# Statistics and normalisation of a stage's first block in the stage before it

## What is computed

```python
x = x + 0.5 * L0_ffn(layernorm(x))    # gated recurrence over the batch, tanh out
x = x + L0_attn(layernorm(x))         # 16 heads, squared softplus scores
x = x + 0.5 * L0_ffn(layernorm(x))    # the same weights again
x = x + 0.5 * L1_ffn(layernorm(x))    # mixture: 8 experts, best 2
x = x + L1_attn(layernorm(x))         # state space layer (SSM)
x = x + 0.5 * L1_ffn(layernorm(x))    # the mixture again

def layernorm(x, eps=1e-05):
    m, v = mean(x, -1), var(x, -1)
    return (x - m) / sqrt(v + eps)

def L0_ffn_step(c, xt):               # c starts as in_c, broadcast
    ft = sigmoid(xt @ wf.T + c @ uf.T + bf)
    it = sigmoid(xt @ wi.T + c @ ui.T + bi)
    gt = tanh(xt @ wc.T + c @ uc.T + bc)
    return ft * c + it * gt

def L1_ffn(x):
    gates = softmax(x @ gate_w.T + gate_b)       # the best 2 of 8 are kept
    return sum(gate * expert(x) for the 2 experts)
```

## Time and profile before

| What | us |
|---|---|
| Median of 3 runs | 1934.23 |
| The profiled execution's own time | 1933.88 |
| Its span, first to last instruction | 1932.1 |
| TensorE busy | 1752.0 (91%) |
| VectorE busy | 1340.6 (69%) |
| ScalarE busy | 1130.9 (59%) |
| GpSimd busy | 901.4 (47%) |

### The profile page before, as it was taken

One profiled execution on the slowest core, in us unless ns is written; L12 is line 12 of the kernel. 1 busy time (PEld: TensorE's weight loads), 2 busy tenths in 40 slices (PEclk: granted clock), 3 DMA queues, 4 the chain that ended last, 5 costly groups with the idle time before them and its releaser, 6 DMA issues. The chain is left out here.

```text
span 1932.1 us, 30828 instructions
## 1 busy us (share of the span) xinstructions
PE 1752.0 (91%) x9742; PEld 1156.5 (60%) x9742; DVE 1340.6 (69%) x2878; ACT 1130.9 (59%) x1624; POOL 901.4 (47%) x654
## 2 busy tenths in 40 slices
PE   5999787999999999997999799997898899989998
PEld 4888673222222222227888677776676676767776
DVE  4545895777777777775555588885677777768886
ACT  3323588999999999994333222213777777622220
POOL 0001116999999999994002232211554445521111
PEclk9999898999999999998999999998999999999999
DMA  4000165534535435300000000001322222300000
GB/s 152 1 0 11 65 186 103 83 44 62 69 43 72 58 46 83 45 1 12 1 0 21 23 17 0 0 0 33 125 89 88 88 88 88 121 2 22 22 21 23
DMA packets 57640, 96.96 MB, mean 50 GB/s; under 512 B 7936, under 2 KB 29664, under 8 KB 57568
## 3 DMA queue, kind: packets, MB, share of 16 engines
q1 hardware_dynamic: 55392, 94.50, 21.7%
q10 hardware_dynamic: 2176, 1.55, 0.2%
HBM read 78.98 MB, written 17.04 MB: 50 GB/s over the span
## 5 line engine op out<-in xcount | busy, mean ns | idle before, releaser
L1232 POOL TENSOR_TENSOR att_weights<-att_weights 128x1024 f32<-128x1024 f32 x288 | 541.0, 1893 | 17.7 <-DVE att_weights L1176 7.3
L1176 DVE SCALAR_TENSOR_TENSOR att_weights<-att_weights,ps 128x512 f32<-128x512 f32 x576 | 370.1, 684 | 152.3 <-ACT att_weights L1152 150.5
L1152 ACT ACTIVATE att_weights<-att_weights 128x1024 f32<-128x1024 f32 x288 | 302.5, 1051 | 0.0
L1148 ACT ACTIVATE att_weights<-ps 128x1024 f32<-128x1024 f32 x288 | 294.1, 1022 | 9.9 <-PE ps L1094 5.6
L720 DVE SCALAR_TENSOR_TENSOR X<-ps,moe_gsel,X 128x256 f32 (+1 forms) x512 | 246.6, 484 | 64.4 <-PE ps L47 48.4
L1108 PE MATMUL ps<-att_weights,att_v_ones 128*32 128x512 f32 (+3 forms) x1536 | 288.8, 497 | 2.6 <-POOL att_weights L1232 2.5
L47 PE MATMUL ps<-w_experts_hi,moe_xh 128*128 128x512 f32 x512 | 205.2, 401 | 0.0
L47 PE MATMUL ps<-w_experts_hi,moe_xl 128*128 128x512 f32 x512 | 203.1, 397 | 0.0
L47 PE MATMUL ps<-w_experts_lo,moe_xh 128*128 128x512 f32 x512 | 201.6, 394 | 0.0
L313 ACT ACTIVATE ffn_gates<-ps,ffn_gate_bias 128x512 f32<-128x512 f32 x96 | 66.1, 688 | 207.2 <-PE ps L47 200.8
L1091 PE MATMUL ps<-q_stack,k_stack 128*128 128x512 bf16 (+3 forms) x384 | 116.8, 341 | 29.5 <-DVE att_weights L1176 19.8
(11 more groups left out here) (257 smaller groups left out, 3881.4 us busy)
## 6 DMA issues: line engine op xcount, KB each, us to landing
ssm_lb<-decays SPq DMA_DIRECT2D x32, 512.0 KB, 4.5
ssm_rise<-decays SPq DMA_DIRECT2D x32, 512.0 KB, 3.8
qk_parts<-qkv_part SPq DMA_DIRECT2D x32, 384.0 KB, 2.6
q_stack<-qk_parts SPq DMA_DIRECT2D x64, 128.0 KB, 4.5
k_stack<-qk_parts SPq DMA_DIRECT2D x64, 128.0 KB, 8.2
att_q_stack<-qk_parts SPq DMA_DIRECT2D x64, 128.0 KB, 4.6
att_k_stack<-qk_parts SPq DMA_DIRECT2D x64, 128.0 KB, 8.0
out<-X SPq DMA_DIRECT2D x8, 512.0 KB, 2.9
```

Source lines behind the costliest of these rows:

```text
L1148: act.activation(Wt[:, u % WU], scores(u), ACT.Exp).then_inc(exp_done, 1)
L1152: act.activation(Wt[:, u % WU], Wt[:, u % WU], ACT.Ln, bias=1.0).then_inc(ln_done, 1)
L1176: dve.scalar_tensor_tensor(out=wt[:, t], in0=wt[:, t], scalar=LIMIT, in1=scores(u)[:, t], op0=ALU.min, op1=ALU.max).then_inc(max_done, 1)
L1232: pool.tensor_tensor(Wt[:, u % WU], Wt[:, u % WU], Wt[:, u % WU], ALU.mult).then_inc(sq_pool, 1)
```

## The change

A new class `Ahead` holds one normalised block (`ahead.xn`), its statistics and its scale for the whole program. That buffer is also slot 0 of every stage's `Norm`. Three stages now fill it at their end for the stage behind: load for the first feed-forward stage, the projection for the second, the state space stage for the last mixture. In those three the stage behind has its own statistics and normalisation of block 0 taken out and counts the semaphores up by hand (`sem_inc`), and its first turn has lead 0 and fill 8. QKV, the first mixture and the state space stage keep theirs.

Cut to its core:

```diff
+class Ahead:
+    def dve_stats(self, dve, x):
+        for j in range(GT):
+            dve.bn_stats(self.stats[:, j], x(j))
+        dve.drain()
+        for j in range(GT):
+            ins = dve.bn_aggr(self.mv[:, j], self.stats[:, j])
+        ins.then_inc(self.mv_done, 1)
+        dve.wait_ge(self.mv_done, 1)
+        dve.tensor_scalar(self.var[:, :], self.mv[:, :, 1], LN_EPS, None, ALU.add).then_inc(self.var_done, 1)
+    def pool_rstd(self, pool):
+        pool.memset(self.power[:, :], -0.5).then_inc(self.power_set, 1)
+        pool.wait_ge(self.power_set, 1)
+        pool.wait_ge(self.var_done, 1)
+        pool.tensor_tensor(self.rstd[:, :], self.var[:, :], self.power[:, :], ALU.pow).then_inc(self.rstd_done, 1)
+    def dve_apply(self, dve, x):
+        dve.wait_ge(self.rstd_done, 1)
+        for j in range(GT):
+            ins = dve.tensor_scalar(self.xn[:, j * C:(j + 1) * C], x(j), self.mv[:, j, 0:1],
+                                    self.rstd[:, j:j + 1], ALU.subtract, ALU.mult)
+        ins.then_inc(self.xn_done, 1)
+        dve.wait_ge(self.xn_done, 1)
...
# ffn_phase, tensor
-            norm.pe_first_turn(pe, norm.var_done, ring[:, 0, 0:P], 6, 5)
+            norm.pe_first_turn(pe, norm.var_done, ring[:, 0, 0:P], 0, 8)
# ffn_phase, vector
-            norm.dve_stats(dve, 0, 0, lambda j: tile_of(0, 0, j))
-            norm.dve_apply(dve, 0, 0, lambda j: tile_of(0, 0, j))
+            for made in (norm.mv_done, norm.var_done, norm.xn_done):
+                dve.sem_inc(made, 1)
...
# load_phase, scalar
-            act.dma_start(mask[:, :], mask_src).then_inc(small_in, 16)
-            act.dma_start(bias_raw[:, :], bias_src).then_inc(small_in, 16)
-            for dst, src in smalls:
-                act.dma_start(dst, src).then_inc(small_in, 16)
             x_tiles = X[:, :].rearrange("p (b t c) -> p b t c", b=B, t=PT)
+            for dst, src in smalls[:3]:
+                act.dma_start(dst, src).then_inc(small_in, 16)
             act.dma_start(x_tiles[:, 0], batches(x_dram)[:, 0]).then_inc(x_in, 16)
+            for dst, src in smalls[3:]:
+                act.dma_start(dst, src).then_inc(small_in, 16)
+            act.dma_start(mask[:, :], mask_src).then_inc(small_in, 16)
+            act.dma_start(bias_raw[:, :], bias_src).then_inc(small_in, 16)
             split.split_hi(act)
# load_phase, vector (the casts and the subtraction of constants go to gpsimd,
# behind ahead.pool_rstd and a wait for the small constants)
+            split.split_lo(dve, 0, len(split.jobs) // 2)
+            dve.wait_ge(x_in, 16)
+            ahead.dve_stats(dve, tile_of)
+            split.split_lo(dve, len(split.jobs) // 2, len(split.jobs))
+            ahead.dve_apply(dve, tile_of)
...
# projection_phase, vector
             lo(GROUPS - 1, 1)
+            dve.wait_ge(x_done, 4 + 2)
+            ahead.dve_stats(dve, tile_of)
             residual(GROUPS - 2, 0)
+            ahead.dve_apply(dve, tile_of)
             residual(GROUPS - 1, 1)
# projection_phase, gpsimd, behind the eight bias additions
+            ahead.pool_rstd(pool)
...
# ssm_phase, vector, group(p, v, left); left is 0 in the last group alone
+                if not left:
+                    dve.wait_ge(x_done, FREE + p * GT)
+                    ahead.dve_stats(dve, next_tile)
                 times_dt(p, v, 0)
                 times_dt(p, v, 1)
                 for b in range(GT):
...
                     if b:
                         residual(p, b - 1)
+                    if not left and b == 1:
+                        ahead.dve_apply(dve, next_tile)
# ssm_phase, gpsimd, behind the first scale_x of the last group
+                    if b == NORM_AT and not left:
+                        ahead.pool_rstd(pool)
...
# moe_phase, vector, without a tail
+                for made in (norm.mv_done, norm.var_done, norm.xn_done):
+                    dve.sem_inc(made, 1)
+                dve.memset(f32(g3[:, :, :, :]), 0.0).then_inc(g3_zero, 1)
# moe_phase, gpsimd, without a tail, in place of scales(0, 0)
+                for made in (norm.rstd_done, neg_done, shift_done):
+                    pool.sem_inc(made, 1)
```

More of the change, by code:

```diff
@@ L70, with __init__ @@
 class Norm:
-    def __init__(self, nc, sb, sem, psum_t, ident, tag, slots=2, parts=None):
+    def __init__(self, nc, sb, sem, psum_t, ident, tag, ahead, slots=2, parts=None):
         self.nc, self.ps, self.ident = nc, psum_t, ident
-        self.xn = sb(f"{tag}_xn", [P, slots, GW], F32)
+        self.xn = [ahead.xn] + [sb(f"{tag}_xn{s}", [P, GW], F32) for s in range(1, slots)]
         self.stats = sb(f"{tag}_stats", [P, slots, GT, 6], F32)
@@ L209, in dve_residual, with ffn_phase @@
                                  op0=ALU.mult, op1=ALU.add).then_inc(self.x_done, 1)
-def ffn_phase(nc, tag, X, ident, ps, W, small, tail, jobs=(), x_dram=None):
+def ffn_phase(nc, tag, ahead, X, ident, ps, W, small, tail, jobs=(), x_dram=None):
     wh, wl = (part.rearrange("p (m k) c -> p m k c", k=KC) for part in W)
@@ L221, in ffn_phase @@
         sem = lambda n: ctx.sem(n)
-        norm = Norm(nc, sb, sem, ps[:, 0:2], ident, tag)
+        norm = Norm(nc, sb, sem, ps[:, 0:2], ident, tag, ahead)
         gates = sb(f"{tag}_gates", [P, KC, 3, GN], F32)
@@ L377, in _ @@
             norm.pool_setup(pool)
-            for s in range(2):
-                norm.pool_rstd(pool, s, s)
+            pool.sem_inc(norm.rstd_done, 1)
+            norm.pool_rstd(pool, 1, 1)
             with pool.Fori(1, GROUPS // 2) as i:
@@ L433, in split_hi, with split_lo @@
             act.activation(hi, self.raw[:, n % self.RAW, 0:src.shape[1]], ACT.Copy).then_inc(self.hi_done, 1)
-    def split_lo(self, dve):
-        for n, (src, hi, lo) in enumerate(self.jobs):
+    def split_lo(self, dve, first, end):
+        for n in range(first, end):
+            src, hi, lo = self.jobs[n]
             dve.wait_ge(self.loaded[n % self.RAW], 16 * (n // self.RAW + 1))
@@ L461, in load_phase @@
         x_in = sem("load_x_in")
+        ahead.open(sem)
         block = ctx.enter_context(nc.Block())
@@ L1359, with ssm_phase @@
 PROJ = 2 * DI + 2 * DS + NH
-def ssm_phase(nc, tag, X, ident, ps, W_in, spare, consts, decay_dram):
+def ssm_phase(nc, tag, ahead, X, ident, ps, W_in, spare, consts, decay_dram):
     wh, wl = W_in
@@ L1374, in ssm_phase @@
         sem = lambda n: sem_(f"{tag}_{n}")
-        norm = Norm(nc, sb_, sem_, ps[:, 0:2], ident, tag, slots=1, parts=spare)
+        norm = Norm(nc, sb_, sem_, ps[:, 0:2], ident, tag, ahead, slots=1, parts=spare)
         tri = sb("tri", [P, P])
@@ L1966, in build @@
         iota = sb("moe_iota", [P, E], F32)
+        ahead = Ahead(sb)
         neg = sb("neg", [P, P], BF16)
@@ L2027, in build @@
                 loaded = [nc.alloc_semaphore(name=f"loaded{n}_{s}") for s in range(2)]
-                qkv_phase(nc, f"qkv{n}", X, ident, ps, weights("qkv", 0, KC, 3 * C), V, parts_dram, tail,
+                qkv_phase(nc, f"qkv{n}", ahead, X, ident, ps, weights("qkv", 0, KC, 3 * C), V, parts_dram, tail,
                           stacks, loaded)
@@ L2033, in build @@
                 sides.close()
-                projection_phase(nc, f"proj{n}", X, ident, ps, weights("proj", 0, KC, C), V, proj_bias)
+                projection_phase(nc, f"proj{n}", ahead, X, ident, ps, weights("proj", 0, KC, C), V, proj_bias)
                 early.close()
@@ L2043, in build @@
             if ph == "S":
-                ssm_phase(nc, f"ssm{n}", X, ident, ps, weights("even", 0, KC, PROJ), weights("even", KC * PROJ, KC, GN),
+                ssm_phase(nc, f"ssm{n}", ahead, X, ident, ps, weights("even", 0, KC, PROJ), weights("even", KC * PROJ, KC, GN),
                           t, decay_dram)
```

76 lines of the change are left out of this document (45 added, 31 removed).

## The result

The changed kernel takes 1943.05 us, the kernel before 1935.66 in the same session (medians of seven runs each): a ratio of 1.0039, with a 95% interval of 1.0027 to 1.0051. It is slower, by about 7 us. The forecast was 1935.4, no difference that can be told; the measured time lies above the range (1929.0 to 1939.5). Of the 7.65 us between forecast and result 1.8 are the starting point: the forecast added to 1933.88, and the kernel before takes 1935.66 here.

The account below looks back on a forecast made before the run. TensorE was taken to bound the kernel, with winnable idle time at stage borders. Terms of -3.15 without the clock and +4.65 for it gave +1.5 on 1933.88, so 1935.4 us; range 1929.0 to 1939.5.

Parts of the forecast that it names:

- Term: 0: Loading: VectorE would end at 18.0 against 18.09, so no gain or loss; ends -1.7 and +3.0.
- the middle of three: Loading: X, issued 3.1 earlier and again taking 9.8, lands at 11.95, between landing early and gaining nothing.
- costed at nothing: Loading: GpSimd's four small operations would fit beside 3.8 us of VectorE, otherwise costing some tenths.
- Term: -1.25: Each feed-forward stage: first product 1.25 us earlier, not 4.7, since ScalarE still fills the state buffers.
- Projection +2.2: Projection's end: statistics and block added to VectorE, which finishes last, cost 2.2 us after 1.5 idle are used.
- Last mixture -4.35: Last mixture: the copy of the logits comes 4.35 us earlier behind the barrier.
- State space stage +1.5: Last group: statistics ahead of the first product with dt delay the chain by 2.14 - 0.63, 1.5 us.
- hidden with some tenths to spare: Last group: the block delays the decay product, but TensorE's tile 3 waits for GpSimd's scaling anyhow; no cost.
- The clock, +4.65: Clock falls after TensorE's pauses: +1.7 in each feed-forward stage, +0.85 in the mixture, +0.4 in the last group.
- half a fall, +0.4: State space stage's last group: a longer pause before TensorE's second turn, on a chain only partly TensorE's, costs 0.4 us.
- +0.85: Last mixture: pauses of 1 to 2 us, close together, cost half a clock fall, 0.85 us.
- The rival of the long falls: Long clock falls in all four places, met by products from the start: 8.5 on -3.15, 1939.2 us; chance 0.13.

Follow-up runs that it names:

- e7: Changed kernel with later places in the state space stage's last group, VectorE making state c, ScalarE's upper halves split, 6 filling products: ratio to before 0.9956.
- e9: e7 plus X loaded in two halves and the projection's statistics of block 0 in three pieces before the last low halves: ratio to before 0.9958.
- e3: Kernel before with only the change's part at loading, feed-forward stages and projection; state space stage and last mixture as before: ratio to before 1.0034.
- e10: Changed kernel with only power and block of the state space stage's last group moved later, statistics left early: one run, 1937.0 us.
- e1: Changed kernel with 21 filling products instead of 8 behind the first turn of both feed-forward stages: ratio to before 0.9999.
- e4: Changed kernel with statistics, power and block at later places in the state space stage's last group: ratio to before 1.0008.
- e8: Changed kernel with 21 filling products in both feed-forward stages, later places in the last group, and X's first quarter in two transfers: ratio to before 0.9976.

## Why the prediction was wrong

- **"Term: 0" for loading** failed: it was +1.85 (first product +0.60 with the stage's own -1.25 kept; by the means of four profiles with the old start and six with the new, 28.3 and 29.3, it is 2.2). I took the middle of three, X at 11.95; it landed at 13.1, which is 1.15 of it. The rest are GpSimd's small operations, "costed at nothing": they made the block 0.67 longer. The weights were late as well, without a cost.
- **"Term: -1.25" for each feed-forward stage** held, and why: ScalarE's state (e7).
- **Projection +2.2** measured +1.74 (from the start of the last low half to the last residual's end: 5.38 before, 7.12 after). Right in kind; the statistics overlap a little more.
- **Last mixture -4.35** measured -4.49.
- **State space stage +1.5**: the statistics alone are 1.2. But "hidden with some tenths to spare" for the block failed: the sum moved the decay product back and left every length as it was. It then ran beside GpSimd's decay and scaling, and that costs 0.9.
- **The clock, +4.65**, is the step that failed most: it measured some 7.7 (2.60 and 2.94 in the feed-forward stages, 2.2 in the last group, nothing in the mixture). I took 1.7 for each feed-forward stage, from a stage whose pause of 2.96 let TensorE work on at 0.66. In the first stage the fall came before the first product, the first 5 us ran at 0.50, and the stage is 2.60 longer. In the second they ran at 0.71, which is worth 1.4; the rest of the 2.94 is the fall near its end, which the sum did not hold at all. All profiles add up in this way: 171.1 to 171.6 (first stage) and 170.8 (second) without a fall, 1.5 to 1.8 more with one near the end, 1.4 to 1.5 more with one at the start at 0.66 to 0.71, 2.4 to 2.8 more with one at 0.50. Of the 14 stages with the pause left open (seven kernels) 12 begin with a fall and 13 have one near the end; of the other 18 one begins with a fall (e9) and six have one near the end. Why those near the end come so often behind an open pause stays open. In the last group, "half a fall, +0.4" was 2.2: its chain hangs on TensorE at tile 0. In the mixture +0.85 did not come at all.

The rival of the long falls, 1939.2, had the mechanism: falls that the products meet from the start. I gave it 0.13, against "part of it would meet filling work". That happened in two of the 14 stages, the second of e3 and of e10, and in neither of the changed kernel's. Of the 3.9 us that it lacks to 1943.05, 1.8 are the starting point. Of the rest, loading adds 1.85 and the last group 1.9 (a larger fall, and the scaling), while the mixture's fall of 1.7 did not come; what is left lies within the interval. The 2.9 of the loop are no part of it: they stand in the profiled execution alone.

The trace disagrees with the Trainium skill, TensorE: Matmul & The Clock Gate, section Why this matters for your kernels, as the forecast already found: it names only pauses longer than these 2.1 as what throttles the array, and here four of five unfilled pauses of 2.1 in the last group were followed by a fall.

## What to carry to other kernels

Work that is taken from in front of TensorE's first product is worth only what the next-slowest chain in front of it leaves, and it opens a pause that can cost more than that: move it only together with what now bounds the start (here the state, e7), or keep TensorE at work up to the first product (e1), for long enough that a fall in front of it is over (in e9 it was not). Where the moved step goes, look for an engine's idle time in that very stage and put it there, as e4 did; the same three steps cost 4.3 us at one place and nothing at another. And when VectorE's work lands beside GpSimd's, price both as longer.

## What the hardware showed that I had not expected

- VectorE and GpSimd slow each other, in two places: block 1.38 alone, 1.90 and 2.05 beside GpSimd; the decay product 1.22 alone (the last group's first), 2.12; GpSimd's scaling 2.49 and 3.47; the cast 0.29 and 0.75. In e1 the decay product ran first and took 1.23, and it was GpSimd's decay of the state that took 2.13 instead of 1.04; the group was as long. The Trainium skill, SBUF — State Buffer, section SBUF: two separate sides, says that the two share a pair of ports, and that a GpSimd instruction, or one of VectorE's that uses both its ports or reads two operands from SBUF, holds it for the whole instruction; the lengths agree: the decay product's 2.12 is about its own 1.22 and the 1.04 of the decay of the state that began with it, and in e1 it is the other way round.
- A 1 MB transfer that is issued 3.1 earlier lands only 1.9 earlier (13.1 for 15.05), and makes the others late: X took 10.8 to 12.1 in the ten profiles with it whole and early, 9.3 to 9.9 in the four with it late, and the weights' median was 5.8 to 8.1 and 5.3 to 5.8. With half of it early VectorE's wait for X was gone (e8, e9).
- Falls of the clock behind pauses of 2.0 to 2.3 us, in the state space stage's loop and near the end of each feed-forward stage, differ from one profile to the next without any change there: 342.7 to 347.3 for the same loop. A single profile compares that loop only to some 4 us; the medians and e3 showed which differences were real.
